# Reading a state-space scan out by four neighbouring tokens per product, with the own columns picked by DMA

## The chip, the cores and the metric

The kernel runs on one NeuronCore of a Trainium2 chip. The metric is the time of one execution on the device in microseconds, the median of several runs. The engines are TensorE (PE, products into PSUM), VectorE (DVE), ScalarE (ACT), GpSimd (POOL) and SyncE (SP, which here only starts DMAs). Each works through its own list of instructions in order and waits on semaphores that the others raise.

## The reference, cut to what matters

Two layers over 2048 tokens of width 256: a selective scan (state space model) and a mixture of experts, then linear attention and a gated network. The change lies in the scan and its read-out. With STATE = 64, for every channel `d` and token:

```
delta = softplus(delta @ dt_proj_w.T + dt_proj_b);  A = -exp(A_log)
c_idx = arange(L) % 64;  C_used = C_ssm[:, c_idx, :]
def step(h, inp):
    dt, b, xt, c = inp
    h = exp(dt[:, :, None] * A) * h + dt[:, :, None] * b[:, None, :] * xt[:, :, None]
    y = einsum('bdn,bn->bd', h, c)          # the read-out
    return (h, y)
...
return (y + x * D_param) @ out_proj_w.T     # the skip term, the projection
```

The result is added to `x`; a router then picks two of eight experts for each token, and the tokens are scattered to the experts' slots. `C_used` depends only on the token's place in its 64 and on the sequence, so one set of read-out weights serves all chunks of a sequence.

## The kernel before

A first part (`prepare`, to about 100 us) norms the tokens, makes the step sizes and inputs and writes them, split into bf16 parts, to HBM. Then `selective_scan` runs over 32 chunks of 64 tokens; a chunk has 8 groups (GROUPS) of 16 channels each in two halves of the 256 channels. One pass of the main loop over groups is called a step here, `gi = 8 c + j`. All engines go through one list that `scan_schedule` writes out:

- `stream`: TensorE makes the decays of group gi+1 (line 884, `rows` times `shared`, which holds the A parts, into `bank_a`) and the inputs of group gi (line 903, `xdiag` times `bstat`, into `bank_in[gi % 2]`), the second once scan gi-2 is done. ScalarE turns the decays into exponentials (line 1014; three buffers, so it waits for scan gi-3) and then writes the carry of the group before it into the inputs (`hand_on`, line 1024). GpSimd makes that carry from the last state of the chunk before (lines 1283, 1289) and clears the first decay. VectorE runs the scan of group gi-2 (line 1128) over 16 channels x 64 tokens, with state and half of the channels on the partitions, into `h`.
- `y`: the read-out of the chunk before. `h` holds, for each of 128 channels, 64 tokens side by side. A product takes one token's column of every channel, 128 f32 that lie 256 bytes apart, against the 32 columns of `cstat` for that token; the 64 tokens of a chunk go in four column strips of TensorE (`q`), and each product adds one token's rows to `bank_y`. There are 16 products in each of the steps j = 2, 4, 6 of a chunk and j = 0 of the next (`Y_STEPS`; LAG = 2 shifts them).
- `TILE_END`, once for a tile of two chunks: `y_out` (ScalarE copies `bank_y` to `y_sb`, line 1063), `yT` (two transposes, line 952, into `bank_z`), `yt` (ScalarE copies to `y_t`), `proj` and `proj2` (lines 929, 930: `y_t` and the skip term `skip_c` times `w_out`), `resid` (VectorE adds `x`, line 1152; SP stores it, line 847, and loads the next tile's `skip_c` and `xres`).
- `first` (line 945) and `first_out`: the first token's input of a chunk, for the carry. `bank_z` is used in turns by `first`, the router and the tile's end; `z` counts them.
- The router's steps for five blocks of tiles (ROUTED) go between, one a step, ending with the scatters (line 1298: GpSimd writes the descriptors). The last two blocks are routed after the scan, with the read-out of the last chunk.
- `load_parts`: SP loads the rows of chunk c+1 in six pieces at steps 0 to 5 (lines 199, 204, 201).

## Time and profile before

| | before |
|---|---|
| median of 3 runs | 1338.55 us (1335.17 to 1338.65) |
| the profiled execution | 1341.49 us, its span 1340.0 us |
| busy in the span | PE 87%, DVE 63%, ACT 36%, POOL 22% |
| scans of VectorE | 256, the first from 101.7 us, the last from 716.3 us |
| first scatter after the scan stage | 738.67 us |

The span is what lies between the first and the last instruction; the execution's own time has 1.5 us more. Times in the rows are microseconds from the start of the span. PEclk is the clock granted to TensorE: 1.00 is 2.4 GHz, 0.50 is 1.2 GHz. An f32 product stands in the profile as two records. A name's buffer number is left out; `psum` is all of PSUM.

### The profile page before, as it was taken

How to read it: one execution, taken by the hardware profiler on the slowest of the kernel's cores; microseconds unless marked ns; L12 is line 12 of the kernel's file. 1: busy time of each engine (PE TensorE's matmuls, PEld its weight loads, DVE VectorE, ACT ScalarE, POOL GpSimd, SP SyncE). 2: the span in 40 equal slices, each digit the busy share in tenths (PEclk: the TensorE clock that was granted, in tenths of full speed). 3: DMA queues.
4: the chain of work that ended last, by engine and by line, in shares of the span. 5: the costliest groups of instructions: out<-in, count | busy, mean ns of one | idle time of the engine just before them, and what ended most of it. 6: DMA issues, size and time to landing. Idle time of an engine off the chain costs nothing.

```text
span 1340.0 us, 35020 instructions
## 1 busy us (share of the span) xinstructions
PE 1162.8 (87%) x14859; PEld 829.2 (62%) x14859; DVE 847.6 (63%) x1006; ACT 484.5 (36%) x1169; POOL 299.6 (22%) x914
## 2 busy tenths in 40 slices
PE   3647898989988899889997499999999597999998
PEld 2435666666666666666665388888777344465665
DVE  5858999999989999899995112121111477742211
ACT  2864555555545555455543111111111110121110
POOL 9641222222241222422232211111111200000000
PEclk9765989889987799798988699999999698999999
DMA  3797245443222122321214642222210400000000
GB/s 105 234 283 219 63 93 132 116 117 88 45 66 55 42 53 52 87 46 36 54 43 158 245 165 99 84 76 84 96 47 12 133 1 0 0 9 8 16 16 16
DMA packets 165757, 110.35 MB, mean 82 GB/s; under 512 B 91653, under 2 KB 156296, under 8 KB 163296
## 3 DMA queue, kind: packets, MB, share of 16 engines
q1 hardware_dynamic: 157168, 86.65, 23.4%
q0 software_dynamic: 8000, 20.87, 4.7%
q8 instruction: 117, 1.92, 0.6%
q10 hardware_dynamic: 432, 0.59, 0.1%
q14 instruction: 40, 0.33, 0.1%
HBM read 63.18 MB, written 45.90 MB: 81 GB/s over the span
## 4 chain that ended last, share of the span: by engine, by line
PE 62%; DVE 14%; issue 7%; ACT 6%; SPq 5%; POOL 2%; DMA 2%; DVEq 0%; POOLq 0%; ACTq 0%
PE psum L917 12%; PE psum L1371 10%; PE psum L1383 10%; PE psum L1855 8%; DVE h L1128 7%; PE psum L903 5%; PE psum L884 5%; PE psum L1866 4%; ACT decay L1014 4%; DVE den L1685 2%; PE psum L1811 2%; POOL disp_d L1298 2%; SPq L199 1%; SPq L278 1%; PE psum L1803 1%
## 5 line engine op out<-in xcount | busy, mean ns | idle before, releaser
L1128 DVE TENSOR_TENSOR_SCAN h<-decay,psum 128x1024 f32<-128x1024 f32 x256 | 570.3, 2272 | 35.9 <-ACT psum L1024 26.7
L1014 ACT ACTIVATE decay<-psum 128x512 f32<-128x512 f32 x512 | 278.6, 597 | 248.3 <-PE psum L884 221.1
L917 PE MATMUL psum<-h,cstat 128*32 128x128 f32 x4096 | 248.1, 395 | 3.1 <-DVE h L1128 3.1
L903 PE MATMUL psum<-xdiag,bstat 96*128 96x64 bf16 x4096 | 184.7, 203 | 12.3 <-DVE h L1128 10.1
L917 PEld LDWEIGHTS psum<-h,cstat 128*32 128x32 f32 x4096 | 140.7, 129 | 58.6 <-DVE h L1128 3.6
L903 PEld LDWEIGHTS psum<-xdiag,bstat 96*128 96x128 bf16 x4096 | 152.1, 104 | 30.9 <-DVE h L1128 15.4
L884 PE MATMUL psum<-rows,shared 32*128 32x64 bf16 x4096 | 115.8, 200 | 55.9 <-ACT decay L1014 47.0
L884 PEld LDWEIGHTS psum<-rows,shared 32*128 32x128 bf16 x4096 | 83.1, 99 | 129.0 <-ACT decay L1014 67.2
L1283 POOL TENSOR_TENSOR carry<-decay,h 128x16 f32<-128x16 f32 x240 | 60.8, 253 | 364.1 <-ACT decay L1014 364.0
L1371 PE MATMUL psum<-xdt,shared 128*128 128x320 f32 x512 | 140.9, 436 | 0.7 <-ACT xdt L1430 0.7
L1383 PE MATMUL psum<-shared,hid 128*128 128x256 f32 x640 | 139.5, 379 | 0.6 <-ACT hid L1424 0.6
L1383 PEld LDWEIGHTS psum<-shared,hid 128*128 128x128 f32 x640 | 121.0, 190 | 17.2 <-issue 1.1
L1371 PEld LDWEIGHTS psum<-xdt,shared 128*128 128x128 f32 x512 | 98.2, 192 | 41.4 <-issue 2.2
L1855 PE MATMUL psum<-xt,wgu 128*128 128x512 f32 x256 | 112.7, 600 | 2.5 <-DVE at L1690 2.5
L1458 DVE TENSOR_SCALAR hid<-psum 128x320 f32<-128x320 f32 x64 | 31.5, 492 | 112.1 <-PE psum L1371 112.1
L1493 POOL DMA_INDIRECT picked_d<-eo,to x40 | 39.2, 980 | 258.4 <-ACT eo L1427 135.6
L1855 PEld LDWEIGHTS psum<-xt,wgu 128*128 128x128 f32 x256 | 49.1, 192 | 64.2 <-issue 59.4
L1461 DVE TENSOR_SCALAR eo<-psum,gate 128x256 f32<-128x256 f32 x20 | 9.7, 484 | 116.9 <-PE psum L1383 111.2
L1708 DVE TENSOR_TENSOR shared<-psum,sil 128x512 f32<-128x512 f32 x32 | 22.0, 691 | 81.5 <-PE psum L1855 81.5
L1424 ACT ACTIVATE hid<-psum 128x320 f32<-128x320 f32 x64 | 28.0, 437 | 118.3 <-PE psum L1371 118.3
L1779 ACT ACTIVATE sil<-psum 128x512 f32<-128x512 f32 x32 | 19.1, 597 | 131.2 <-PE psum L1855 127.1
L1289 POOL TENSOR_TENSOR carry<-carry,u 128x16 f32<-128x16 f32 x240 | 53.0, 221 | 24.9 <-ACT u L1050 4.4
(191 smaller groups left out, 1068.7 us busy)
## 6 DMA issues: line engine op xcount, KB each, us to landing
shared<-in_w SPq DMA_DIRECT2D x16, 1024.0 KB, 5.0
xdiag<-x_parts_d SPq DMA_DIRECT2D x256, 48.0 KB
x_parts_d<-x_parts POOLq DMA_DIRECT2D x46, 256.0 KB, 7.8
parts_d<-dt_parts SPq DMA_DIRECT2D x24, 256.0 KB, 8.4
rows<-parts_d SPq DMA_DIRECT2D x128, 48.0 KB
disp_d<-zero SPq DMA_DIRECT2D x4, 1305.0 KB, 8.2
xd<-disp_d SPq DMA_DIRECT2D x8, 652.5 KB, 6.2
picked_d<-zero SPq DMA_DIRECT2D x4, 1024.0 KB, 5.4
```

The source lines that it names most:

```text
L884: ins = pe.q.matmul(bank_a[half][:, i * T:(i + 1) * T], s["astat"][strip, RCH * g + q, :], rows[strip, c % 2, q, :], start=True, stop=True)
L903: ins = pe.q.matmul(to.rearrange("p d (s e) -> p s d e", e=2), bstat[0:ROWS, c % 2, b, :], xdiag[0:ROWS, c % 2, b, :, d, :], start=True, s ...
L917: ins = pe.q.matmul(bank_y[32 * q:32 * q + 32, P * (c % CT):P * (c % CT + 1)].rearrange("p (s d) -> p s d", s=2), s["cstat"][:, tok, :], h ...
L1014: act.q.activation(decay[:, gi % NB, 8 * half:8 * half + 8, :], per_d(bank_a[half]), ACT.Exp).then_inc(sem("exp"), 1)
L1128: dve.q.tensor_tensor_scan(out=h[:, half_slot(c, half), ch:ch + G, :].rearrange("p d t -> p (d t)"), data0=decay[:, gi % NB, :, :].rearran ...
L1283: pool.q.tensor_tensor(whole, first, h[:, half_slot(c - 1, half), ch:ch + G, T - 1], ALU.mult).then_inc(sem("carry_made"), 1)
L1289: pool.q.tensor_tensor(whole.rearrange("p (h i) -> p h i", h=2), whole.rearrange("p (h i) -> p h i", h=2), own, ALU.add).then_inc(sem("car ...
L1371: ins = pe.q.matmul(table.bank(key)[:, 0:half_cap], w1[:, e % 2, dh, f * P:(f + 1) * P], xdt[:, e % 2, dh, c * half_cap:(c + 1) * half_cap ...
L1383: ins = pe.q.matmul(table.bank(key)[:, 0:D], hid[:, e % 2, f, st * P:(st + 1) * P], w2[:, e % 2, f, :], start=f == 0, stop=f == FT - 1)
L1493: pool.q.indirect_dma_start(out=s["picked_d"], out_offset=bass.IndirectOffsetOnAxis(ap=to[:, e, st:st + 1], axis=0), in_=eo[:, e % 2, st, ...
L1855: ins = pe.q.matmul(table.bank(key)[:, :], wgu[:, j, dh, f * P:(f + 1) * P], xt[:, u, dh, :], start=dh == 0, stop=dh == 1)
L1866: ins = pe.q.matmul(table.bank(key)[:, 0:D], gt[:, blk % 2, f, n * P:(n + 1) * P], wd[:, f, :], start=f == 0, stop=f == FT - 1)
```

## The change

The read-out takes four neighbouring tokens at a time: the moving operand is `h[..., tok:tok+4]`, 512 columns (2 halves x 64 channels x 4 tokens), and `cstat` has 32 columns for a group of four tokens instead of for one. A chunk has 16 such products, four in each of the same four steps, and they fill the whole bank. Of the output only the columns of a row's own token are wanted: row 16 dh + 4 j + e of a strip wants columns e. ScalarE copies all columns, once a chunk, to `y_raw` with the four tokens apart, and four DMAs from SP (`y_sel`) take partitions e, e+4, ... of part e to `y_sb`. The last chunk is picked by products with columns of the identity instead. The read-out of a chunk now waits until the bank of the chunk before is copied. The skip term is added to `y_t` by GpSimd in place of two of the four products of the projection. The tile's end moves: for tile i, counted from step 16 (i + 1), `yT` goes from step 11 to 13, `yt` from 12 to 14, `proj` from 13 to 17, `resid` from 15 to 19 (15 and 17 for tile 14); `first` is always at the end of the chunk before. The router's uses of `bank_z` get other steps (5 in even chunks, 1 and 3 in odd), its weights are worked out before its ranks, and in the last four chunks it may do two steps at a time.

```
-            s |= dict(cmat=sb("cmat", [P, BATCH, CSPAN]), cstat=sb("cstat", [P, CSPAN, 32]),
+            s |= dict(cmat=sb("cmat", [P, BATCH, CSPAN]), cstat=sb("cstat", [P, CSPAN // 4, 32]),
...
-Y_STEPS = ((0, 1, 2, 3), (), (4, 5, 6, 7), (), (8, 9, 10, 11), (), (12, 13, 14, 15))
-TILE_END = ((0, "y_out"), (2, "yT"), (3, "yt"), (4, "proj"), (4, "proj2"), (6, "resid"))
+Y_SEL = 16 * 4
+Y_STEPS = ((0,), (), (1,), (), (2,), (), (3,))
+Y_OUT, Y_PICK = 7, 8
+TILE_END = ((4, 4, "yT"), (5, 5, "yt"), (8, 6, "proj"), (8, 6, "proj2"), (10, 8, "resid"))
...
-            if any(name in Z_WRITE for name, *args in steps[0]) and (ending or open_z or j not in ((1, 3, 5), (1,))[c % 2]):
+            if any(name in Z_WRITE for name, *args in steps[0]) and (ending or open_z or j not in ((5,), (1, 3))[c % 2]):
...
+        if c >= CHUNKS - 4 and routing and not any(name in AT_PACE for name, *args in routing[0][1][0]):
+            yield from advance(c, j)
...
+        for at, what in ((Y_OUT, "y_out"), (Y_PICK, "y_sel")):
+            ended, rest = divmod(gi - LAG - GROUPS - at, GROUPS)
+            if rest == 0 and 0 <= ended < CHUNKS - 1:
+                yield (what, ended)
+        for at, at_last, what in TILE_END:
+            for i in range(TILES - 1):
+                if gi == GROUPS * (CT * (i + 1)) + LAG + Y_OUT + (at if i < TILES - 2 else at_last):
+                    yield from finish(i, what)
...
+                elif kind == "y_sel":
+                    c = x[0]
+                    sp.wait_ge(sem("y_out"), c + 1)
+                    if c >= CT:
+                        sp.wait_ge(sem("yT"), c // CT)
+                    for e in range(4):
+                        sp.q.dma_start(y_sb[e:P:4, c % CT, :], y_raw[e:P:4, c % CT, e, :]).then_inc(sem(f"y_sel{c % CT}"), 16)
...
-                    if c >= CT:
-                        pe.wait_ge(sem("y_out"), c // CT)
+                    pe.wait_ge(sem("y_out"), c)
...
-                        tok = 16 * q + j
-                        ins = pe.q.matmul(bank_y[32 * q:32 * q + 32, P * (c % CT):P * (c % CT + 1)
-                                                 ].rearrange("p (s d) -> p s d", s=2),
-                                          s["cstat"][:, tok, :], h[:, first:last + 1:last - first, :, tok],
-                                          start=j == 0, stop=j == 15)
+                        tok = 16 * q + 4 * j
+                        ins = pe.q.matmul(bank_y[32 * q:32 * q + 32, :].rearrange("p (s d e) -> p s d e", s=2, e=4),
+                                          s["cstat"][:, tok // 4, :], h[:, first:last + 1:last - first, :, tok:tok + 4],
+                                          start=j == 0, stop=j == 3)
...
-                pe.q.matmul(bank_z[:, 0:256], y_t[:, dh, :], w_out[:, dh, :], start=dh == 0, stop=False)
-                ins = pe.q.matmul(bank_z[:, 0:256], skip[:, c % 2, dh, :], w_out[:, dh, :], start=False, stop=dh == 1)
+                ins = pe.q.matmul(bank_z[:, 0:256], y_t[:, dh, :], w_out[:, dh, :], start=dh == 0, stop=dh == 1)
...
+                    for half in range(2):
+                        at = half_slot(c, half) > half_slot(c, 1 - half)
+                        part = bank_y[:, 256 * at:256 * at + 256].rearrange("p (b a i e) -> p a e b i", a=2, i=8, e=4)
+                        for n in range(2):
+                            ins = act.q.copy(y_raw[:, c % CT, :, 64 * half + 32 * n:64 * half + 32 * n + 32
+                                                   ].rearrange("p e (b i) -> p e b i", i=8), part[:, n])
...
+                elif kind == "yt":
+                    c, z = x
+                    pool.wait_ge(sem("z_free"), z + 1)
+                    pool.wait_ge(sem(f"skip_ld{c % 2}"), 16 * (c // 2 + 1))
+                    both = y_t[:, :, :].rearrange("p h t -> p (h t)")
+                    pool.q.tensor_tensor(both, both, skip[:, c % 2, :, :].rearrange("p h t -> p (h t)"), ALU.add
+                                         ).then_inc(sem("skip_added"), 1)
```

TensorE's list around the end of tile 0, before. Line 884 is the decays, 903 the inputs, 917 the read-out, 952 the transposes:

```order
L903 MATMUL psum<-xdiag,bstat 128x4x8x2 x16
L952 MATMUL psum<-ident,y_sb 128x128 x2
L884 MATMUL psum<-rows,shared 128x64 x16
L903 MATMUL psum<-xdiag,bstat 128x4x8x2 x16
L917 MATMUL psum<-h,cstat 32x128 x16
L884 MATMUL psum<-rows,shared 128x64 x16
L903 MATMUL psum<-xdiag,bstat 128x4x8x2 x16
L929 MATMUL psum<-w_out,y_t 128x256
L930 MATMUL psum<-w_out,skip_c 128x256
L929 MATMUL psum<-w_out,y_t 128x256
L930 MATMUL psum<-w_out,skip_c 128x256
L884 MATMUL psum<-rows,shared 128x64 x16
```

And in the changed kernel, from right behind the two transposes of the same tile (its lines are 902 for the decays, 921 the inputs, 935 the read-out, 961 `first`, 946 the projection):

```order
L902 MATMUL psum<-rows,shared 128x64 x16
L921 MATMUL psum<-xdiag,bstat 128x4x8x2 x16
L935 MATMUL psum<-h,cstat 32x512 x4
L902 MATMUL psum<-rows,shared 128x64 x16
L921 MATMUL psum<-xdiag,bstat 128x4x8x2 x16
L961 MATMUL psum<-xdiag,bstat 128x128
L902 MATMUL psum<-rows,shared 128x64 x16
L921 MATMUL psum<-xdiag,bstat 128x4x8x2 x16
L935 MATMUL psum<-h,cstat 32x512 x4
L902 MATMUL psum<-rows,shared 128x64 x16
L921 MATMUL psum<-xdiag,bstat 128x4x8x2 x16
L946 MATMUL psum<-w_out,y_t 128x256 x2
```

The projection stood two steps behind the transposes and stands four behind them now, in the next chunk, with half the products.

SP's list over an odd and the next even chunk, before. Lines 199, 204 and 201 load the rows of the next chunk, 847 stores the residual of a tile, 829 and 831 load for its next but one:

```order
L199 DMA rows<-parts_d 12x32x64 x4
L204 DMA bstat<-b_parts_d 48x8x64 x2
L201 DMA xdiag<-x_parts_d 12x8x256 x8
L847 DMA x_d<-x1o 128x256
L829 DMA skip_c<-skip_d 128x2x128
L831 DMA xres<-in_x 128x256
L199 DMA rows<-parts_d 12x32x64 x4
L204 DMA bstat<-b_parts_d 48x8x64 x2
L201 DMA xdiag<-x_parts_d 12x8x256 x8
```

And an even chunk of the changed kernel (865 is `y_sel`, 858 the residual's store, 840 and 842 the two loads):

```order
L199 DMA rows<-parts_d 12x32x64 x4
L204 DMA bstat<-b_parts_d 48x8x64 x2
L865 DMA y_sb<-y_raw 32x128 x4
L201 DMA xdiag<-x_parts_d 12x8x256 x2
L858 DMA x_d<-x1o 128x256
L840 DMA skip_c<-skip_d 128x2x128
L842 DMA xres<-in_x 128x256
L201 DMA xdiag<-x_parts_d 12x8x256 x6
```

The store, which waits for the residual, stood behind all loads of a chunk and stands between the second and the third xdiag load now, and the picks, which wait for ScalarE's copy, stand ahead of them.

TensorE's list behind the last inputs of the scan stage, before and then changed (975 and 997 transpose the router's tiles, 985 and 1007 are its logits):

```order
L917 MATMUL psum<-h,cstat 32x128 x48
L975 MATMUL psum<-ident,r_xl 128x128 x6
L917 MATMUL psum<-h,cstat 32x128 x32
L985 MATMUL psum<-r_wg,r_xt 128x8 x2
L952 MATMUL psum<-ident,y_sb 128x128 x2
```

```order
L946 MATMUL psum<-w_out,y_t 128x256 x2
L935 MATMUL psum<-h,cstat 32x512 x12
L997 MATMUL psum<-ident,r_xl 128x128 x6
L935 MATMUL psum<-h,cstat 32x512 x8
L1007 MATMUL psum<-r_wg,r_xt 128x8 x2
L970 MATMUL psum<-ident,y_sb 128x128
L974 MATMUL psum<-ident,y_raw 128x32 x4
```

The order of the tail is the same; the second transpose has become four products with columns of the identity.

## Rows read from the trace of the kernel before

**Rows 1.** The page: its first line and VectorE's scan among the groups.

```profile
span 1340.0 us, 35020 instructions
...
L1128 DVE TENSOR_TENSOR_SCAN h<-decay,psum 128x1024 f32<-128x1024 f32 x256 | 570.3, 2272 | 35.9 <-ACT psum L1024 26.7
```

**Rows 2.** Busy time of the engines, 130 to 700 us, with clock.

```profile
core 0: us, PE busy (x) PEld busy (x) DVE busy (x) ACT busy (x) POOL busy (x), PEclk, DMA share, GB/s
130.00:700.00 570.00, 515.49 (x11696) 375.18 (x11697) 546.25 (x382) 308.99 (x851) 155.73 (x716) 0.89 0.30 71
```

**Rows 3.** Groups of instructions, 130 to 700 us: busy, mean ns, idle before.

```profile
L1014 ACT ACTIVATE decay<-psum 128x512 f32<-128x512 f32 x478 | 260.1, 598 | 232.3 <-PE psum L884 211.8 <-DVE h L1128 19.3
L917 PE MATMUL psum<-h,cstat 128*32 128x128 f32 x3816 | 230.9, 395 | 0.0
...
L1024 ACT COPY psum<-carry 128x16 f32<-128x16 f32 x230 | 44.8, 195 | 6.3 <-POOL carry L1289 6.3
...
L1063 ACT COPY y_sb<-psum 128x64 f32<-128x64 f32 x60 | 8.4, 227 | 20.7 <-PE psum L917 20.7
L1050 ACT COPY u<-psum 128x128 f32<-128x128 f32 x29 | 8.2, 284 | 0.2 <-PE psum L945 0.2
```

**Rows 4.** VectorE's timeline: start, us, instruction, idle before it.

```profile
189.16 19.86 DVE L1128 TENSOR_TENSOR_SCAN h<-decay,psum 128x1024 f32<-128x1024 f32 x9 [0.61 <-ACT psum L1024]
```

**Rows 5.** VectorE's timeline while scatters are written, first and last of four.

```profile
391.87 2.29 DVE L1128 TENSOR_TENSOR_SCAN h<-decay,psum 128x1024 f32<-128x1024 f32 x1 [1.19 <-ACT psum L1024]
...
401.96 6.64 DVE L1128 TENSOR_TENSOR_SCAN h<-decay,psum 128x1024 f32<-128x1024 f32 x3 [1.05 <-ACT psum L1024]
```

**Rows 6.** Timeline of TensorE over a read-out step, clock 1.00.

```profile
386.40 0.64 PE L903 MATMUL psum<-xdiag,bstat 96*128 96x64 bf16 x16
...
386.97 1.93 PE L917 MATMUL psum<-h,cstat 128*32 128x128 f32 x32
...
388.83 0.41 PE L884 MATMUL psum<-rows,shared 32*128 32x64 bf16 x16
```

**Rows 7.** The same over a read-out step at clock 0.50, with ScalarE.

```profile
404.39 1.01 PE L903 MATMUL psum<-xdiag,bstat 96*128 96x64 bf16 x16 [0.82 <-DVE h L1128]
...
405.33 1.95 PE L917 MATMUL psum<-h,cstat 128*32 128x128 f32 x32
...
407.21 0.61 PE L884 MATMUL psum<-rows,shared 32*128 32x64 bf16 x16
...
407.86 1.09 ACT L1014 ACTIVATE decay<-psum 128x512 f32<-128x512 f32 x2 [2.43 <-PE psum L884]
```

**Rows 8.** Busy time by stretch; columns as in rows 2.

```profile
402.60:412.90 10.30, 8.90 (x176) 6.91 (x176) 10.01 (x5) 3.64 (x8) 0.50 (x4) 0.50 0.44 96
412.90:429.90 17.00, 14.58 (x373) 10.41 (x369) 16.06 (x9) 10.13 (x26) 2.90 (x16) 1.00 0.19 41
```

**Rows 9.** Other f32 products: timeline of line 1383, group of line 1855.

```profile
777.64 17.43 PE L1383 MATMUL psum<-shared,hid 128*128 128x256 f32 x80
...
L1855 PE MATMUL psum<-xt,wgu 128*128 128x512 f32 x256 | 112.7, 600 | 2.5 <-DVE at L1690 2.5
```

**Rows 10.** Timeline of TensorE behind the last scan: the last read-out.

```profile
718.65 3.69 PE L917 MATMUL psum<-h,cstat 128*32 128x128 f32 x64 [3.07 <-DVE h L1128]
...
723.64 3.67 PE L917 MATMUL psum<-h,cstat 128*32 128x128 f32 x64
```

**Rows 11.** Groups of GpSimd over the whole span.

```profile
L1605 POOL TENSOR_TENSOR x<-xb,brow 128x256 f32<-128x256 f32 x16 | 11.1, 720 | 59.6 <-DVE xb L1620 59.6
```

**Rows 12.** SP's timeline: issues, start and us.

```profile
400.93 0.34 SPq L847 DMA_DIRECT2D x_d<-x1o  x1
...
402.95 1.80 SPq L199 DMA_DIRECT2D rows<-parts_d  x4
...
406.07 4.37 SPq L201 DMA_DIRECT2D xdiag<-x_parts_d  x8
```

**Rows 13.** DMA issues, 380 to 440 us: KB each, us to landing.

```profile
x_d<-x1o SPq DMA_DIRECT2D x1, 128.0 KB, 2.4
```

More of the change, by code:

```diff
@@ L655, in router_steps @@
     yield [("mm_last", n - 1)]
-    yield from ([(name,)] for name in (*CHOOSE, "rank", *WEIGH, *SETTLE, "count"))
+    yield from ([(name,)] for name in (*CHOOSE, *WEIGH, "rank", *SETTLE, "count"))
     for i in range(n):
@@ L662 @@
 Z_DONE = {v: x for x, v in Z_WRITE.items()}
+AT_PACE = {*Z_WRITE, *Z_DONE, "scatter"}
 def scan_schedule():
@@ L673, in stamp @@
         if name in Z_WRITE:
+            assert not open_z
             open_z = True
@@ L710, in scan_schedule @@
             starts = j == 0 and c % CPB
-            if starts and c % 2 == 0:
-                yield stamp("first", c)
             yield ("stream", gi)
@@ L722, in scan_schedule @@
             yield ("y", c_read, Y_STEPS[step])
-        for at, what in TILE_END:
-            ended, rest = divmod(gi - LAG - GROUPS - len(Y_STEPS) - at, GROUPS * CT)
-            if rest == GROUPS * (CT - 1) and 0 <= ended < TILES:
-                yield from finish(ended, what)
-        if j == GROUPS - 1 and c % 2 == 0:
+        for at, what in ((Y_OUT, "y_out"), (Y_PICK, "y_sel")):
[6 more added lines that the diff above has]
+                    yield from finish(i, what)
+        if j == GROUPS - 1 and (c + 1) % CPB and c + 1 < CHUNKS:
             yield stamp("first", c + 1)
@@ L1032, in place_c @@
                     cst = s["cstat"][r, :, :].rearrange("p (q j) c -> p q (j c)", q=4)
-                    ins = act.q.copy(cst[:, :, dh:dh + 34 * 15 + 1:34],
-                                     s["cmat"][r, b, :].rearrange("p (q j) -> p q j", q=4))
+                    for e in range(4):
+                        at = 16 * dh + e
+                        ins = act.q.copy(cst[:, :, at:at + 36 * 3 + 1:36],
+                                         s["cmat"][r, b, :].rearrange("p (q j e) -> p q j e", q=4, e=4)[:, :, :, e])
                 ins.then_inc(sem("c_placed"), 1)
```

52 lines of the change are left out of this document (27 added, 25 removed).

## The prediction

> **What bounds the kernel now.** I first read the page: the span is 1340.0 us, and the scan instruction of VectorE (line 1128, 256 of them) is the costliest group, 570.3 us [rows 1]. The reader is to see that it is nearly gapless and that what is missing is small: over the whole run VectorE sat idle 35.9 us ahead of its scans, 26.7 of them until ScalarE had handed a carry on (line 1024). Then the busy time of the scan stage: from 130 to 700 us VectorE is busy 546 of 570 us, TensorE 515, ScalarE 309, and the mean granted clock of TensorE is 0.89 [rows 2]. So two engines are close to their limit, and the groups say which instructions fill TensorE: the read-out of line 917 alone is 230.9 us, 3816 records in steps of 32, 119 steps, while ScalarE stands idle 232 us ahead of its exponentials, nearly always for TensorE [rows 3]. Third the timeline of VectorE: nine scans without a gap take 19.86 us, 2.2 us a step [rows 4]. 256 steps at that pace are 563 us. The stage cannot get under that; the change can only win what VectorE idles.
>
> How much of the 26.7 us belongs to TensorE? In the stretch where GpSimd writes scatter descriptors, four waits of VectorE follow one another, the first 1.19 and the last 1.05 us [rows 5], 4.1 us in all; there are three such stretches in the scan stage, one for each routed block, 12.3 us, and the change leaves their eight descriptors each as they are. That leaves 26.7 - 12.3 = 14.4 us. This is all that a shorter read-out can win in the scan stage.
>
> Why TensorE makes VectorE wait is seen in one step with a read-out in it. When a scan ends, TensorE may do the inputs (line 903) of the next buffer, then the read-out, then the decays (line 884), then ScalarE its two exponentials and the hand-over, and that must be there two steps, 4.4 us, later. At the full clock, 2.4 GHz, inputs to read-out is 386.40 to 386.97, read-out to decays 386.97 to 388.83, decays 0.41 [rows 6]; with 1.09 for the exponentials [rows 7] and 0.2 for the hand-over (line 1024, [rows 3]): 0.57 + 1.86 + 0.41 + 1.09 + 0.2 = 4.13 us, in time. At a granted 0.5, 1.2 GHz, the same is 0.94 + 1.88 + 0.65 (407.21 to 407.86) + 1.09 + 0.2 = 4.76 us [rows 7]: 0.36 us too late. That is what the waits are. A mean of 0.89 means that 22% of the stage ran at the low level; 22% of 128 read-out steps, 28, times 0.36 is 10 us, and the remaining 4 us I give to the 15 tile ends, where four products of line 929 and 930 come on top.
>
> **The change, part by part.** *The products.* Before, a step issues 16 products of 128 columns, in four column strips side by side, two records each: eight rounds in 1.93 us. The last record takes 0.39, so a round is (1.93 - 0.39) / 7 = 0.22 us for 128 columns, 1.7 ns a column. It is the same 0.22 at 1.2 GHz (1.95 us for 32 records) [rows 6, 7], while line 903 goes from 0.64 to 1.01. So these products are not bound by the clock at 2.4 GHz. Other f32 products, with their columns side by side, take 17.43 / 80 = 0.218 us for 256 columns, 0.85 ns a column [rows 9]. What sets line 917 apart is that its moving operand takes one f32 of each 256 bytes. Now it takes four neighbours. I take the row of the 256 columns for the new pace, because the new operand has runs of four: 512 columns 0.436 us a round, two rounds a step, the last record 0.60 as for line 1855 [rows 9]: 0.436 + 0.60 = 1.04 us in place of 1.93. The other end: the old pace per column stays, 512 columns 0.87 us, two rounds 1.9 us, nothing won. At 1.2 GHz both ends give about 1.9: the 0.85 ns a column of 2.4 GHz doubled is the 1.7 that line 917 has already.
>
> The Trainium skill ("Advanced Engine Details and Errata", SBUF Cachelines) says that SBUF lines are 16 bytes and that a read needs at least two hits in a line for full bandwidth. By that the 0.22 us is the penalty and the new round would be 0.43 us; without it the step would stay at 1.9 us. The trace agrees with the first half only: the old pace is half of the others'.
>
> *What it is worth.* At 2.4 GHz the path of a read-out step falls from 4.13 to 0.57 + 1.04 + 0.41 + 1.29 = 3.3 us, so a stall there needs most of that path to lie at 1.2 GHz. At 1.2 GHz it stays at 4.76. So everything hangs on how often the clock is low. It fell in the trace after stretches in which TensorE had gaps, and came back after 402.6 to 412.9, a dense stretch at 0.5 [rows 8]. Two products of 256 columns are four records, 4 x 0.218 = 0.9 us [rows 9]. The change takes 0.85 us from each of 119 read-out steps between 130 and 700 and 0.9 from each of 14 tile ends, 114 of 515 busy us: TensorE then has gaps in every pair of steps, at about 70% busy. I take it that the clock falls twice as often, 44% of the stage. A low stretch now hurts only where it covers inputs, read-out and decays together; I take 20 steps of 128 (16%), 20 x 0.36 = 7.2 us. The bounds: 0, and all 56 steps (44%), 20.2 us.
>
> The Trainium skill ("TensorE: Matmul & The Clock Gate", Part 1: The HAM clock gate) says that the throttled clock is the default and activity releases it. That speaks against a change that empties TensorE while VectorE sets the pace; by it the low share grows. The sum above does without it.
>
> *Tile end.* Two products instead of four (line 929, 930), on a step without read-out; won: the 4 us named above, already inside the 14.4; 0 if those waits were others'. *ScalarE.* Four copies of 128 columns per chunk instead of four of 64 per tile; Four of the old are 8.4 / 15 = 0.56 us; of the new size one is 0.284, so four are between 0.56 x 284 / 227 = 0.70 and 4 x 0.284 = 1.14, and I take 0.8: 32 x 0.8 - 16 x 0.56 = 17 us more, against 232 us idle [rows 3]. Queued behind them are the next exponentials. At 2.4 GHz the earlier end of the read-out covers that; at 1.2 it adds 0.15 us on perhaps 7 of 32 chunk ends: 1 us. *GpSimd.* An addition of 128x256 is 0.72 us [rows 11], 16 times. It waits for ScalarE's y_t copies while the next carry stands behind it; but that carry waits for the next exponentials, which come 2 us later, so 0. Without this cover it would be 11.5 us. *DMA picks.* 4 x 31 transfers on SP; a transfer of 128 KB lands in 2.4 us [rows 13], and the transposes now come four steps (8.8 us) after the copy: 0. If it is late, TensorE stops in the transposes and the decays behind them. *Order.* The wait of a read-out for the copy of the chunk before it: the copy is two steps ahead, 0. The doubled router steps of the last chunks are VectorE instructions that are only moved: 0. *Tail.* The last chunk's read-out is 3.69 + 3.67 us [rows 10], the first half at 1.2 GHz: that stays, the second becomes 3 x 0.436 + 0.60 = 1.9, minus 1.8. Two products fewer, minus 0.9; the addition, plus 0.7; larger copy and five instead of two transposes, plus 0.6; the residual of tile 14 now behind the last scan, plus 0.4: together minus 1.0.
>
> Sum: -14.4 + 7.2 + 1.0 - 1.0 = -7.2 us. Against its own time of 1341.49 (span 1340.0 and 1.5 around it) the profiled execution gives 1334.3. It lay 2.9 above the median of the runs, 1338.55; on that: **1331.4 us**.
>
> **Rivals.** (1) *The clock holds.* For it: 412.9 to 429.9 stayed at 1.00 with TensorE at 86% [rows 8]. Against it: that is before the emptying. Then the 7.2 and the 1.0 fall away: 1323. (2) *The rate per column stays*, since four strips may share one read path. For it: line 917 is the only group with column strips, too. Then only the tile ends win, -4, with +1 for ScalarE, and the tail is +0.8: 1336.4. (3) *The clock turns it round.* Place: inputs, read-out and decays at 1.2 GHz in most read-out steps. Price 0.36 each; it decides from 14.4 / 0.36 = 40 such steps in 128. With all 56: +20.2 - 14.4 + 1 - 1 = +5.8, 1344. Against it: a dense stretch at the low level brought the clock back [rows 8]. (4) *The loads come late.* In even chunks SP now waits for the residual of the tile with six of eight xdiag loads behind it. From the end of scan 8c-3, the residual is due at 4 x 2.2 + 0.45 = 9.2 us; its store and two loads take 2.0 (400.93 to 402.95), six loads 6/8 of 4.37, 3.3 [rows 12], landing 2.4: 17. The first reader of that data, line 945, stands at 8 x 2.2 + 0.6 = 18.2. So 1 us of room, 15 times. It decides once the data lands 1.5 us later than reckoned, 15 x 0.5 = 7.5 us against the 7.2; at 2 us later, 15 - 7 = +8: 1346. (5) *The waits have other causes* (GpSimd's carry, say): the change does what it says and nothing moves, 1339.
>
> **How the numbers follow.** Forecast 0.33, (1) 0.24, (2) 0.18, (3) 0.10, (4) 0.10, (5) 0.05. No change is 0.3% of 1338.55, 4 us: 1334.5 to 1342.6. Of the forecast 0.26 lies under 1334.5, 0.06 within, 0.01 above; of (2) 0.04 under and 0.14 within: faster 0.26 + 0.24 + 0.04 = 0.54; same 0.06 + 0.14 + 0.05 = 0.25; slower 0.01 + 0.20 = 0.21. The forecast's own range is 1326 to 1338. The range of all: from 1319, (1) with the tail wholly at 2.4 GHz (another 1.8) and some of the 12.3 us of scatter waits eased, to 1345, past the end of (3); about 0.1 each way is left out.
>
> **What would show it.** Right: eight records of the read-out in about 1.0 us at 2.4 GHz; a mean clock under 0.85 between 130 and 700; VectorE's idle ahead of its scans down by some 6 us, with waits left where the clock is low and where scatters are; ScalarE's copies four to a chunk at 0.8 us. Wrong: a step of 1.7 us or more at 2.4 GHz (2); a clock of 0.89 or above with the idle down by 14 (1); waits of line 945's successor for xdiag (4); idle above 35.9 with a clock near 0.75 (3).

## The result: slower by 1%

The changed kernel took 1351.88 us (median; 1350.23 to 1355.77) beside 1338.60 of the kernel before: a ratio of 1.0107, 95% interval 1.0078 to 1.0137. Timed once more, in the square of four kernels below, it took 1348.20 beside 1340.24: 1.006 (1.0038 to 1.0082). Both times the whole interval lies above 1.003, so the change costs something, between 8 and 13 us in the medians; the forecast was 1331.4, and 1351.88 lies outside the range to 1345. The profiled execution took 1350.97 us. Medians and ratios are over the fast runs (a ratio is not the quotient of the two medians), and two slow ones of a single kernel below, of 1858 and 3501 us, are left out.

The page of the changed kernel, its span, clock and scan, which answer to [rows 1]:

```profile
span 1349.1 us, 29055 instructions
...
PEclk8865868776888779876877599999999797999999
...
L1151 DVE TENSOR_TENSOR_SCAN h<-decay,psum 128x1024 f32<-128x1024 f32 x256 | 568.6, 2269 | 41.9 <-ACT psum L1046 34.5
```

VectorE's idle time ahead of its scans was to fall by some 6 us and rose by 6.0, from 35.9 to 41.9. From the first scan to the end of the last the stage took 622.2 us; it had taken 616.9. So 5.3 of the profiled execution's 9.5 us lie there, and 3.3 between the last scan and the first scatter (23.42 us in place of 20.08).

The busy times between 130 and 700 us, columns as in [rows 2]:

```profile
130.00:700.00 570.00, 474.86 (x8688) 275.24 (x8685) 538.64 (x379) 319.59 (x903) 160.54 (x720) 0.79 0.31 73
```

TensorE is busy 41 us less, where the prediction reckoned with 114 us, and its granted clock went from 0.89 to 0.79. The groups of the same stretch, columns as in [rows 3]; the first row is the inputs of the kernel before, the others are the changed kernel:

```profile
L903 PE MATMUL psum<-xdiag,bstat 96*128 96x64 bf16 x3816 | 168.2, 201 | 10.1 <-DVE h L1128 8.0 <-issue 1.0
...
L1036 ACT ACTIVATE decay<-psum 128x512 f32<-128x512 f32 x471 | 257.0, 601 | 197.4 <-PE psum L902 102.6 <-DVE h L1151 94.3
...
L921 PE MATMUL psum<-xdiag,bstat 96*128 96x64 bf16 x3772 | 180.6, 209 | 53.9 <-DVE h L1151 52.6
L935 PE MATMUL psum<-h,cstat 128*32 128x512 f32 x940 | 172.6, 815 | 0.0
...
L1088 ACT COPY y_raw<-psum 128x128 f32<-128x128 f32 x116 | 22.4, 280 | 34.9 <-PE psum L935 34.9
```

Three things are to be seen. The read-out went from 230.9 us to 172.6, 58 less where 101 were reckoned, and the inputs, the same products as before, now take 180.6 in place of 168.2. ScalarE's idle time ahead of its exponentials used to be TensorE's doing, 211.8 of 232.3; now 94.3 of 197.4 end with a scan: in many steps TensorE is done early and the scan is what all wait for. And TensorE, too, now waits 52.6 us for scans ahead of its inputs; it was 8.0. These are the gaps that the prediction spoke of.

The read-out step on TensorE's timeline, once at 2.4 GHz and once at 1.2 GHz (start, us, instruction; compare [rows 6, 7]):

```profile
228.95 1.06 PE L935 MATMUL psum<-h,cstat 128*32 128x512 f32 x8
...
237.02 1.94 PE L935 MATMUL psum<-h,cstat 128*32 128x512 f32 x8
```

Of the 124 read-out steps that have all eight records, 59 lie wholly at 2.4 GHz (median 1.065 us), 42 wholly at 1.2 GHz (1.936), 20 see the clock fall inside the step (1.65) and 3 see it rise.

The start of a chunk between 226 and 240 us: TensorE, then VectorE, then SyncE's queue.

```profile
230.54 0.64 PE L921 MATMUL psum<-xdiag,bstat 96*128 96x64 bf16 x16 [0.19 <-DVE h L1151]
235.41 0.29 PE L961 MATMUL psum<-xdiag,bstat 12*128 12x128 bf16 x1 [4.23 <-DMA xdiag<-x_parts_d]
235.41 0.71 PE L902 MATMUL psum<-rows,shared 32*128 32x64 bf16 x16
236.05 1.03 PE L921 MATMUL psum<-xdiag,bstat 96*128 96x64 bf16 x16
```

```profile
228.19 6.64 DVE L1151 TENSOR_TENSOR_SCAN h<-decay,psum 128x1024 f32<-128x1024 f32 x3 [0.21 <-ACT psum L1046]
237.46 2.29 DVE L1151 TENSOR_TENSOR_SCAN h<-decay,psum 128x1024 f32<-128x1024 f32 x1 [2.62 <-ACT psum L1046]
```

```profile
222.04 0.36 SPq L858 DMA_DIRECT2D x_d<-x1o  x1
222.44 0.58 SPq L840 DMA_DIRECT2D skip_c<-skip_d  x1
223.08 0.60 SPq L842 DMA_DIRECT2D xres<-in_x  x1
223.72 1.64 SPq L201 DMA_DIRECT2D xdiag<-x_parts_d  x4
225.71 0.57 SPq L875 DMA_DIRECT2D disp_d<-zero  x1
226.33 2.01 SPq L201 DMA_DIRECT2D xdiag<-x_parts_d  x2
```

TensorE stands 4.23 us before `first`, because the last two xdiag loads were issued at 226.33 to 228.34 behind the residual's transfers and behind a write of zeros of 1305 KB (8.2 us to landing, by the page). While TensorE waits, the DMA engines are full, and the clock falls inside the wait (columns as in [rows 2]: granted clock, DMA share and GB/s come last):

```profile
227.50:234.20 6.70, 3.16 (x79) 1.86 (x75) 6.49 (x4) 2.89 (x8) 1.41 (x7) 1.00 1.02 207
234.40:244.40 10.00, 8.61 (x121) 4.67 (x123) 6.13 (x4) 4.44 (x14) 2.10 (x11) 0.50 0.18 36
```

VectorE loses 2.62 us by it, and when TensorE goes on at the low clock the inputs take 1.03 in place of 0.64, the read-out 1.94. The table of waits between 130 and 700 us has three such places (us in total, number of waits, the longest):

```profile
DVE h L1151 <- ACT psum L1046: 30.4, 43, 2.6
...
PE psum L961 <- DMA xdiag<-x_parts_d: 7.8, 3, 4.2
```

Before, the last was 0.5 us. The window flatters the kernel before, whose longest such wait, 3.9 us, lies at 120 us: over the whole span TensorE waited 4.4 us for xdiag before and 10.9 us in the changed kernel. The two places that are new, at 194 and 235 us, each stand behind a write of zeros of 1305 KB that was issued at most 10 us earlier. Last the tail, TensorE and then SyncE's queue, which answers to [rows 10]:

```profile
724.04 1.92 PE L935 MATMUL psum<-h,cstat 128*32 128x512 f32 x16 [0.99 <-ACT y_raw L1088]
...
727.73 1.92 PE L935 MATMUL psum<-h,cstat 128*32 128x512 f32 x16
729.58 0.61 PE L1007 MATMUL psum<-r_wg,r_xt 128*128 128x8 f32 x4
733.42 0.45 PE L970 MATMUL psum<-ident,y_sb 128*128 128x128 f32 x1 [3.23 <-DMA y_sb<-y_raw]
733.66 1.76 PE L974 MATMUL psum<-ident,y_raw 128*128 128x32 f32 x8
...
736.74 2.08 PE L946 MATMUL psum<-w_out,y_t 128*128 128x256 f32 x4 [0.51 <-POOL y_t L1321]
```

```profile
719.86 1.94 SPq L887 DMA_DIRECT2D shared<-in_w  x4
723.44 0.33 SPq L858 DMA_DIRECT2D x_d<-x1o  x1
723.92 2.38 SPq L865 DMA_DIRECT2D y_sb<-y_raw  x4
```

The read-out of the last chunk is as short as forecast (1.92 for sixteen records). But the pick of the chunk before it (line 865) is issued behind four loads of expert weights of 1024 KB each, and TensorE waits 3.23 us for it. What follows it runs at the low clock again.

### The profile page after: what moved, and what is told of

It is laid out like the page before. It is cut to its first block, busy times and chain, and to the rows that moved or that the text cites. A ratio compares the mean times of both kernels' runs of the same rounds, so it can differ in the third digit from the quotient of the medians.

```text
span 1349.1 us, 29055 instructions
## 1 busy us (share of the span) xinstructions
PE 1126.4 (83%) x11730; PEld 726.6 (54%) x11730; DVE 846.0 (63%) x1006; ACT 500.5 (37%) x1245; POOL 306.3 (23%) x930
## 4 chain that ended last, share of the span: by engine, by line
PE 52%; DVE 21%; issue 9%; SPq 7%; ACT 5%; DMA 3%; POOL 2%; DVEq 0%; POOLq 0%; ACTq 0%
DVE h L1151 13%; PE psum L1401 10%; PE psum L1413 10%; PE psum L1885 8%; PE psum L935 5%; PE psum L1896 4%; PE psum L921 4%; ACT decay L1036 3%; PE psum L902 3%; DVE den L1715 2%; PE psum L1841 2%; SPq L278 2%; DMA xdiag<-x_parts_d 1%; SPq L201 1%; SPq L199 1%
## 5 line engine op out<-in xcount | busy, mean ns | idle before, releaser
L1151 DVE TENSOR_TENSOR_SCAN h<-decay,psum 128x1024 f32<-128x1024 f32 x256 | 568.6, 2269 | 41.9 <-ACT psum L1046 34.5
L921 PE MATMUL psum<-xdiag,bstat 96*128 96x64 bf16 x4096 | 199.9, 211 | 59.3 <-DVE h L1151 57.9
L921 PEld LDWEIGHTS psum<-xdiag,bstat 96*128 96x128 bf16 x4096 | 166.0, 109 | 86.7 <-DVE h L1151 77.3
L902 PEld LDWEIGHTS psum<-rows,shared 32*128 32x128 bf16 x4096 | 90.0, 104 | 221.2 <-issue 114.2
L935 PE MATMUL psum<-h,cstat 128*32 128x512 f32 x1024 | 187.2, 814 | 1.0 <-ACT y_raw L1088 1.0
L902 PE MATMUL psum<-rows,shared 32*128 32x64 bf16 x4096 | 123.9, 207 | 46.5 <-ACT decay L1036 38.0
L1306 POOL TENSOR_TENSOR carry<-decay,h 128x16 f32<-128x16 f32 x240 | 57.9, 241 | 366.6 <-ACT decay L1036 366.4
L1896 PE MATMUL psum<-wd,shared 128*128 128x256 f32 x256 | 56.1, 380 | 1.1 <-DVE shared L1738 1.1
```

Of the source, the lines that this page charges most:

```text
L902: ins = pe.q.matmul(bank_a[half][:, i * T:(i + 1) * T], s["astat"][strip, RCH * g + q, :], rows[strip, c % 2, q, :], start=True, stop=True)
L921: ins = pe.q.matmul(to.rearrange("p d (s e) -> p s d e", e=2), bstat[0:ROWS, c % 2, b, :], xdiag[0:ROWS, c % 2, b, :, d, :], start=True, s ...
L935: ins = pe.q.matmul(bank_y[32 * q:32 * q + 32, :].rearrange("p (s d e) -> p s d e", s=2, e=4), s["cstat"][:, tok // 4, :], h[:, first:last ...
L1151: dve.q.tensor_tensor_scan(out=h[:, half_slot(c, half), ch:ch + G, :].rearrange("p d t -> p (d t)"), data0=decay[:, gi % NB, :, :].rearran ...
L1306: pool.q.tensor_tensor(whole, first, h[:, half_slot(c - 1, half), ch:ch + G, T - 1], ALU.mult).then_inc(sem("carry_made"), 1)
L1896: ins = pe.q.matmul(table.bank(key)[:, 0:D], gt[:, blk % 2, f, n * P:(n + 1) * P], wd[:, f, :], start=f == 0, stop=f == FT - 1)
```

## The experiments

The two theories. **Clock**: TensorE emptied of work runs at 1.2 GHz twice as often, and the read-out steps at that level give back what the others win. **Places**: the moved instructions and the picks cost by where they stand in the queues, whatever the clock does. "before" is the kernel before, timed beside each set. The sets below were timed on different chips. Four kernels were timed twice, in different sets: the changed one (1.0107 and 1.006), the one with late weights (1.0111 and 1.0038), the one with zeros (1.0045 and 0.9992) and the one with both, which alone agrees (0.9968 and 0.9973). So a difference of some 6 to 10 us between kernels of different sets, even taken beside "before", can come from the set alone; only kernels of one set compare more closely.

### Expert weights behind the last pick

```
-        if gi == TOTAL - 1:
-            yield ("load_experts",)
...
     yield ("y_sel", CHUNKS - 2)
+    yield ("load_experts",)
```

> Only one line of SP's order is moved: the loads of the experts' weights (4 MB) go behind the last pick of the read-out instead of ahead of it. If the last pick is late because its packets queue behind the weights, TensorE's 3.2 us wait for y_sb behind the scan stage falls to under 1 us and the time falls by 2 to 3 us, to about 1349. If the pick is late for its own latency, the wait stays at 3 us and the time at 1352.

Measured: 1354.59 (1349.68 to 1363.50), ratio 1.0111 (1.0056 to 1.0167). The first scatter came 20.11 us behind the last scan in place of 23.42, so the wait for the pick is gone. The time did not fall to the 1349 expected; the four times lie 14 us apart, too far to show 3 us. The square of four kernels below measures it.

### The residual's transfers behind the xdiag loads

SyncE's list is put in another order: line 858 and the two loads behind it are held until the chunk's eight xdiag loads are issued.

> On SP the residual's store and the two loads with it go behind all eight xdiag loads of the chunk, as they stood before the change. If late xdiag loads are what costs, the waits of the first-token product for xdiag (7.8 us in three places) go and with them 5 us or more, since each also lets the clock fall: 1346. If the clock falls anyway, for want of work, only the waits' own share goes, 2 to 4 us, and the mean clock between 130 and 700 us stays near 0.79.

Measured: 1352.77, 1.0094 (1.0067 to 1.012); clock in the stage 0.79. TensorE waited 5.7 us for xdiag between 130 and 700 us, in place of 7.8, and over the whole span 9.6 in place of 10.9. The residual's place explains about 2 us of those waits and nothing that shows in the time; in this kernel the picks (3.38 us of issue at 217.01) and the write of zeros still stand ahead of the last ones.

### The old read-out in the new order

```
-Y_STEPS = ((0,), (), (1,), (), (2,), (), (3,))
+Y_STEPS = ((0, 1, 2, 3), (), (4, 5, 6, 7), (), (8, 9, 10, 11), (), (12, 13, 14, 15))
```

with the products, copies and transposes of before, without picks; GpSimd's skip term and all new places stay.

> The moved tile end, the router's new steps, the skip term on GpSimd and the doubled router steps stay, but the read-out is the old one (64 products of 128 columns a chunk, two chunks to a bank, one copy a tile, no picks). If the read-out is what costs (clock theory: TensorE has too little to do between steps), this is faster than both, since it keeps the clock near 0.89 and has two products fewer at the tile end: 1330 to 1338. If the moved tile end and SP's order cost, it is as slow as the changed kernel, 1348 to 1353.

Measured: 1344.86, 1.004 (1.0022 to 1.0057); clock in the stage 0.88. That lies between the two forecasts: 4.5 us over before come without the new read-out and at the old clock.

### Products of zeros in the steps without read-out

```
+        if 0 <= c_read < CHUNKS - 1 and step in (1, 3, 5):
+            yield ("fill",)
...
+                    for _ in range(4):
+                        for q in range(4):
+                            pe.q.matmul(bank_y[32 * q:32 * q + 32, :], s["zero"][:, 0:16].bitcast(BF16),
+                                        s["zero"][:, 0:256].bitcast(BF16), start=False, stop=False)
```

> The changed kernel with 16 idle products more (zeros times zeros in bf16, 512 columns, added to the read-out's bank) in three of the four steps of a chunk that have no read-out: more work for TensorE and nothing else. Clock theory: the mean clock between 130 and 700 us rises from 0.79 to 0.87 or more, VectorE's idle ahead of its scans falls from 42 to about 30 us and the time falls by 8 to 12 us although work was added. Place theory (late loads, copies behind the read-out at a chunk's start): the time stays or rises by a few us.

Measured: 1345.27, 1.0045 (1.0021 to 1.0069); clock in the stage 0.94. Work was added to TensorE, and the kernel is faster than the two others of its set with the new read-out (1354.59 and 1352.77). One forecast failed: VectorE's idle time ahead of its scans was to fall to about 30 us and is 43.7 in this profiled execution (1349.02 us, above the median). The square below has the same kernel again.

### The last quarter of the read-out a step earlier

`Y_STEPS` is `((0,), (), (1,), (), (2,), (3,))`; copies and picks stay.

> The changed kernel with the fourth part of each read-out one step earlier (steps 0, 2, 4, 5 in place of 0, 2, 4, 6), the copies of y_out and the picks where they were. Theory A (ScalarE's copies stand behind a late read-out at a chunk's start and hold the next exponentials): VectorE's waits at chunk starts shrink, 2.62 us between the first two scans of a chunk go back towards 2.26, 32 x 0.2 = 5 to 6 us less, about 1346. Theory B (the low clock makes every pair of steps late, wherever the copy stands): granted clock in the stage stays near 0.79, two read-out steps in a row may even add a little, 1352 to 1354.

Measured: 1350.42, 1.0069 (1.0044 to 1.0095), clock in the stage 0.81. The interval overlaps with both timings of the changed kernel, so no effect is shown; the wait of ScalarE's copies (34.9 us before) is gone, the stage of the profiled execution is not shorter (626.9 us). Theory A has no support.

### GpSimd's skip term alone, in the kernel before

Lines 929 and 930 become two products in place of four, and GpSimd's addition is put ahead of them; nothing else.

> The kernel before with one part of the change alone: GpSimd adds the skip term and each tile's projection has two products instead of four; read-out, places and router steps are the old ones. The prediction's step (4 us of waits at 15 tile ends, 0.9 us of TensorE each, tail minus 0.9 plus 0.7): 1336. If those waits were not the projection's: 1340 (no change) with a granted clock in the stage of 0.88 to 0.89. If GpSimd's addition stands in the way of the carries: above 1343.

Measured: 1337.46, 0.9971 (0.995 to 0.9992), clock 0.88. This part of the change is a gain of 3.4 us, near the 4 that were forecast for it.

### The new read-out with the ends of tiles put back

`TILE_END` is `((3, 3, "yT"), (4, 4, "yt"), (5, 5, "proj"), (5, 5, "proj2"), (6, 6, "resid"))`, the router's slots and line 961 are at their old places. Counted from there, the transposes and the projection come one step later than before, since the picks need it.

> The changed kernel with the tile's end, the router's slots and the first inputs at their old places; the new read-out with its DMA picks and GpSimd's skip term stay. If the moves cost what the kernel with the old read-out and the new places cost (4.5 us): 1352 - 4.5 = 1347, with the clock in the stage still 0.79 to 0.80 and the wait for the last pick behind the expert weights (3.3 us) still there. If the moves are free under the new read-out and all of it is the clock and the tail: 1352. If the new read-out needs the later places (transposes wait for picks): above 1354 with waits of TensorE for the DMA of y_sb.

Measured: 1369.91, 1.021 (1.0169 to 1.025). Far slower than the forecasts of 1347 and 1352, and in the scan stage TensorE never waits for `y_sb`, which the third forecast named. The last kernel below shows the likely reason: one step later than before is a step with a read-out in it. VectorE waits 15.6 us, at 14 tile ends, for the projection.

### The same with zeros and late expert weights

> The kernel of old places with two additions: the expert weights are issued behind the last chunk but one's pick, and TensorE does 16 small products of zeros in each of three steps per chunk without read-out, which add nothing to any sum. If the three costs are separate (places 4.5, tail 3.3, clock 7 of the 13 over before): 1352 - 4.5 - 3.3 - 7 = 1337, a clock in the stage of 0.93 or more. If the filler itself fills the steps that the places need: 1342 to 1345. If the clock doesn't matter: 1344 (places and tail alone).

Measured: 1342.63, 1.0024 (1.0001 to 1.0046), clock 0.95. Against the kernel above 27 us less, of which the tail is 3. The scan interval at the overfull step fell from a mean of 3.71 us to 3.25 only, which is 7 us over 16 tiles; the rest of the gain is spread over the other steps.

### The first inputs of even chunks put back

```
+            if starts and c % 2 == 0:
+                yield stamp("first", c)
             yield ("stream", gi)
...
-        if j == GROUPS - 1 and (c + 1) % CPB and c + 1 < CHUNKS:
+        if j == GROUPS - 1 and c % 2 == 0:
```

> The changed kernel with the first inputs of even chunks (line 961) back at the start of the chunk, one step later; all else as changed. Theory A (the moves cost because this product now waits for xdiag, and because it stands in the pair of steps that also has the copies of y_raw): waits for xdiag fall from 7.8 to under 2 us, the first interval of even chunks from 2.62 towards 2.3: 4 to 6 us less, 1346 to 1348. Theory B (the low clock makes chunk starts late wherever the product stands): 1351 to 1353.

Measured: 1345.92, 1.0055 (1.0033 to 1.0077). Beside 1.006 for the changed kernel that is no difference, beside 1.0107 it would be one. The waits for xdiag were 10.5 us, not under 2, so theory A's mechanism is refuted; whether the place is worth anything stays open.

### Zeros and late weights, without and with that place

> The changed kernel with the 16 products of zeros in three steps per chunk and the expert weights issued behind the last chunk but one's pick. If clock and tail are separate terms: 1345.3 - 3.3 - (the 1.5 us by which that kernel's tail was longer still) = 1341 to 1342, the first scatter 20.1 us behind the last scan. If the filler holds the last chunks' work back: 1344 to 1345.

> Old place of the first inputs, products of zeros, expert weights late, all together. If each term stands by itself: 1352 - 5 (place) - 7 (clock) - 3.3 (tail) = 1337, 3 to 4 us faster than the kernel before. If place and clock are one and the same loss: 1341, as without the place.

Measured: 1334.79, 0.9968 (0.9947 to 0.999), and 1334.10, 0.9973 (0.9954 to 0.9993), beside 1338.99. Both are faster than before, by 4.2 and 4.9 us in the medians; the place of line 961 makes no difference that shows.

### Zeros in the kernel before

GpSimd's skip term in the kernel before, with 32 products of zeros of 128 columns in three steps per chunk.

> The kernel before with GpSimd's skip term (1337.5) and in each of three steps per chunk without read-out 32 products of zeros of 128 columns. If the low clock costs the kernel before, too, as the 0.36 us of the prediction in some 20% of the read-out steps: clock in the stage from 0.88 to 0.95 or more, 4 to 8 us less, 1330 to 1333. If TensorE has no room for it next to the old read-out: 1340 or above.

Measured: 1346.03, 1.0066 (1.0041 to 1.0091): 7 us over before, and 8.6 over the same kernel without the zeros (1337.46, in another set), although the clock in the stage rose from 0.88 to 0.93. TensorE is busy 538 of 570 us there. A high clock is worth nothing by itself; that the products found no room is the likely reason and was not tested further.

### The square: weights and zeros, each without and with

The changed kernel, the first edit, the fourth, and both, timed side by side.

> The changed kernel once more, as the corner of a square of four kernels timed side by side. If its loss doesn't hang on the chip: 1.0107 of before, 1351 to 1354; if it does: anything from 1343 to 1356.

> The changed kernel with the expert weights behind the last chunk but one's pick. The wait of TensorE for that pick in the tail is 3.2 us in the trace: 3.3 us less than the first corner. If the weights also collide with loads of the last chunks: more than 5 us less.

> The changed kernel with 16 products of zeros in three steps per chunk. Clock theory: 8 us or more less than the first corner, at a clock in the stage of 0.94; tail with the wait for the pick as before. If the clock is not what costs: the same as the first corner, or slower by the added work.

> Both edits. If the terms are separate and the first three corners measure as above: first corner - 3.3 - 8 = 1340 to 1341. If the clock's term is as large as the kernel of both edits gave on another chip (0.9968): 1335, and then the third corner should be near 1338.

| kernel | us | ratio to before (1340.24) | clock in the stage |
|---|---|---|---|
| changed | 1348.20 | 1.006 (1.0038 to 1.0082) | 0.80 |
| weights late | 1344.73 | 1.0038 (1.0024 to 1.0053) | 0.79 |
| zeros | 1339.82 | 0.9992 (0.9972 to 1.0012) | 0.95 |
| both | 1336.01 | 0.9973 (0.9955 to 0.9991) | 0.95 |

The terms add: late weights are worth 3.5 and 3.8 us, zeros 8.4 and 8.7. With zeros alone the change's whole loss is gone. In the profiled executions the scan stage shortens by more than that, from 622.6 to 608.8 us, while what follows the last scan takes 4.8 us longer (629.0 for 624.2). The stage of that kernel, in the same stretch, and its scan on the page:

```profile
130.00:700.00 570.00, 491.47 (x10269) 273.44 (x10262) 546.60 (x383) 325.45 (x918) 170.48 (x737) 0.95 0.31 74
```

```profile
L1159 DVE TENSOR_TENSOR_SCAN h<-decay,psum 128x1024 f32<-128x1024 f32 x256 | 566.1, 2266 | 31.6 <-ACT psum L1054 25.2
```

VectorE idles 31.6 us ahead of its scans in place of 40.6 in the changed kernel of the same set. TensorE's timeline shows the products of zeros (line 962) in the gap between inputs and decays, with the read-out after them at 1.07:

```profile
202.29 1.05 PE L962 MATMUL psum<-zero 128*32 128x512 bf16 x16
203.27 0.41 PE L904 MATMUL psum<-rows,shared 32*128 32x64 bf16 x16
203.61 0.64 PE L923 MATMUL psum<-xdiag,bstat 96*128 96x64 bf16 x16
204.18 1.07 PE L937 MATMUL psum<-h,cstat 128*32 128x512 f32 x8
```

The waits for xdiag are as long as ever in this kernel (10.1 us; 9.8 in the changed kernel of the same set):

```profile
PE psum L969 <- DMA xdiag<-x_parts_d: 10.1, 4, 3.9
```

so the 8 us are not won at the late loads.

### The two moves apart, under the old read-out

The first takes the old read-out in the new order and puts line 961's place back, the second puts the ends of tiles back, in the table of the kernel of 1369.91.

> The old read-out in the changed kernel's order (1344.9), with the first inputs of even chunks back at the chunk's start. If that product, which waits for xdiag 8.6 us in three places at its new place, is the move that costs: 1338 to 1340, its waits under 2 us. If it is the tile's end: 1344 to 1345.

> The old read-out in the changed kernel's order, with the tile's end and the router's slots back at their old places and the first inputs of even chunks at their new one. If the tile's end is the move that costs (its stall goes from two steps to the chunk starts): 1338 to 1340. If the first inputs: 1344 to 1345. If both must go back: both kernels at 1341 to 1343.

Measured: 1351.04, 1.0072 (1.0045 to 1.0099), and 1372.70, 1.0234 (1.0211 to 1.0257). Neither comes near 1337.5, and neither forecast held. The first is 11.5 us over before where the kernel of 1344.86, which differs from it only in line 961's place, was 4.5 over in another set: either the old place is worse or the sets differ, and no run here tells which. The second shows what a step too many means. TensorE, then VectorE (938 is the projection, 926 the read-out, 1160 the residual's addition):

```profile
454.59 0.64 PE L912 MATMUL psum<-xdiag,bstat 96*128 96x64 bf16 x16
455.16 1.92 PE L926 MATMUL psum<-h,cstat 128*32 128x128 f32 x32
457.01 1.13 PE L938 MATMUL psum<-w_out,y_t 128*128 128x256 f32 x4
458.08 0.41 PE L893 MATMUL psum<-rows,shared 32*128 32x64 bf16 x16
```

```profile
454.40 2.29 DVE L1136 TENSOR_TENSOR_SCAN h<-decay,psum 128x1024 f32<-128x1024 f32 x1 [0.27 <-ACT psum L1032]
458.18 0.42 DVE L1160 TENSOR_TENSOR x1o<-psum,xres 128x256 f32<-128x256 f32 x1 [1.49 <-PE psum L938]
458.52 2.28 DVE L1136 TENSOR_TENSOR_SCAN h<-decay,psum 128x1024 f32<-128x1024 f32 x1
```

The projection stands behind a read-out, and the addition that needs it stands ahead of the next scan in VectorE's list: 1.49 us of idle VectorE, 4.12 us from scan to scan. The mean interval at this place of the tile is 4.04 us, in place of 2.23 in the kernel of 1344.86, the same one with the new ends: 29 us over 16 tiles, as much as the whole distance of 28 between the two kernels' medians. The clock is high there (0.64 for the inputs), so this step is overfull at 2.4 GHz. So my table tested a third place and not the old one, and the test of the old place under the new read-out was not made.

## Why the prediction was wrong, step by step

**The pace of the new products: right.** 1.065 us at 2.4 GHz (forecast 1.04), 1.936 at 1.2 GHz (1.9). Rival (2) is refuted. In the trace 512 columns in runs of four take 0.45 us a round at 2.4 GHz, 0.88 ns a column for 1.7 before. The rule of the Trainium skill ("Advanced Engine Details and Errata", SBUF Cachelines), full pace only where reads hit one line of 16 bytes again, agrees with both.

**The clock: level right, worth wrong.** 0.78 was forecast, 0.79 came. The old read-out in the new order has 0.88, the new one 0.79, and products of zeros brought it to 0.95, so it is the emptier TensorE that lowers the clock. The rule of the Trainium skill ("TensorE: Matmul & The Clock Gate", Part 1: The HAM clock gate), that the throttle is the default and activity releases it, agrees.

The step that failed is "I take 20 steps of 128 (16%), 20 x 0.36 = 7.2 us". Wholly low were 42 of 124, beyond the 40 at which rival (3) decides, and 20 more were low in part. The prediction had the low share of the stage double, to 44%, and yet let fewer steps be hit than the 28 that it counted before. At the low clock the step is as long as ever (1.94 us), so each low step still costs, and low steps came about as often as the low clock itself: 34% of the steps wholly and 19% in part, at 42% of the time. By 0.36 a step 42 steps are 15 us, all of the 14.4 to be won.

The traces show the balance. Each scan's idle time is put down here to the read-out step that started last before it:

| | before | changed |
|---|---|---|
| steps wholly at 1.2 GHz, idle behind them | 21, 11.0 us | 42, 27.3 us |
| steps wholly at 2.4 GHz, idle behind them | 86, 14.0 us | 59, 2.0 us |

At 2.4 GHz the short read-out did win, 12 us of idle time, some of it because there are fewer such steps. At 1.2 GHz 16 us came on top, since twice as many steps lay there at 0.52 to 0.65 us each and not 0.36. The waits that other things cause (late loads, scatters) are in these sums too. The square shows the same from the other side: raising 0.80 to 0.95 is worth 8.4 us, more than 7.2 for only three quarters of the way to 1. So rival (3) named the mechanism; its 1344 lacked the two terms that follow.

**"Order ... 0", "Tile end": wrong, by about 8 us as far as two sets can be compared.** The prediction gave the moved instructions no price. The old read-out in the new order is 4.5 us over before (interval 3 to 8), the skip term alone 3.4 under it (1 to 7), in another set; what is left between them, 7.9 us, belongs to the new places, at equal clock (0.88). The scan's pace by place in the tile shows a shift: the means of the two steps in which the old tile ends stood went from 2.85 and 2.75 us to 2.22 and 2.30 in the changed kernel, 17 us over 16 tiles, far more than the 4 that the prediction gave to tile ends. All other steps together rose by 22 us, the two chunk starts most, 2.26 to 2.62 and 2.31 to 2.49. That sum has the low clock in it too; in the old read-out at its clock of 0.88 the same two steps take 2.23 and 2.37 and the chunk starts 2.53 and 2.55, so the shift comes with the places. The late xdiag loads are one part that the trace shows (10.9 us of TensorE's waits over the span in place of 4.4), so rival (4) happened, but in few places and not in fifteen, at writes of zeros that it hadn't reckoned with. Its own price, 1346, lay outside the stated range to 1345. Freeing the loads from the residual shortened the waits by about 2 us, and the old place of line 961 not at all. What else the 7.9 us are isn't settled.

**"DMA picks: 0": wrong in the tail.** In the stage they hid. Behind the last scan the pick of chunk 30 stood behind 4 MB of expert weights: 3.23 us of wait, 3.5 and 3.8 us of time in the square. "Minus 1.0" for the tail became plus 3.3. With the weights late the first scatter comes 19.30 us behind the last scan, 0.8 before the 20.08 of the kernel before, so the rest of the tail's sum held.

**Skip term: right.** Minus 3.4 (the interval of the ratio is 0.995 to 0.9992), forecast 4; GpSimd's addition takes 0.72 us. ScalarE's four copies are 22.4 / 29 = 0.77 us (0.8). Rival (5), that nothing moves, is refuted by the skip term's gain and by that of the zeros.

The account from before to changed, from the medians beside before: skip term -3.4, new places +7.9, late pick +3.5, the new read-out by itself 0 (8.0 - 4.5 - 3.5, for the second timing of the changed kernel). By the first timing, 13.3 over before, that last term is 5 us. Only the late pick and the worth of the zeros come from kernels timed side by side; the other terms are estimates across sets. By the same kind of estimate the new read-out at the high clock is worth about 9 us: with zeros and late weights the kernel is 4.2 under before, and the old read-out in the same order was 4.5 over it. The low clock takes that back. Why the sets differ stays open: the kernel before has nearly the same median in all of them (1338.6 to 1340.9), the changed ones do not.

## What to carry to other kernels

Before shortening work on TensorE while another engine sets the pace, price the same steps at 1.2 GHz, and count as many of them there as the low share of the clock says after the change, not fewer. If a shorter instruction is worth nothing at the low clock, cheap products in the gaps can make it pay; in a kernel with 538 of 570 us busy they did not. A stall taken out of one step of a pipeline can come back in others, as 17 us came back as 22 here, so judge a move by the pace at every place of the period; and look at what large transfers stand ahead of each small one in a queue, at the end above all.

## What was not expected of the hardware

Products of zeros, 1440 records and 96.9 us of TensorE's time in the stage, made the kernel faster by 8.4 us, although they only added work. And the short read-out gained at one clock level alone: 1.93 to 1.06 us a step at 2.4 GHz, but 1.95 to 1.94 at 1.2 GHz. Loads of 48 KB issued behind a write of zeros of 1305 KB, while the DMA share was 1.02, held TensorE for 4.23 us.
